# Row gathers that wait for TensorE's matrix products, and a six-tile lag of the adds into node sums

## The reference, cut to what matters

```python
alpha = jnp.einsum('ehd,hd->eh', h_src, a_src) + jnp.einsum('ehd,hd->eh', h_dst, a_dst)
enc = jax.nn.relu(edge_attr @ edge_W.T + edge_b).reshape(-1, H, D)
alpha = alpha + jnp.sum(enc * h_dst, axis=-1)
```

```python
for l in range(L):
    xl = h @ W[l] + b[l]
    ee = edge_attr @ We[l] + be[l]
    msg = norm * jax.nn.relu(xl[row] + ee)
    agg = jnp.zeros_like(xl).at[col].add(msg)
    conv = agg + jax.nn.relu(xl + root[l]) / deg[:, None]
```

## Time and profile before

| | us |
|---|---|
| median of 3 runs | 6056.12 |
| lowest, highest | 6053.90, 6076.91 |
| the profiled execution | 6070.75 |
| its span in the profile | 6069.0 |
| of it edge_scores, first to last gather | 64.8 to 855.2 |
| of it attention_sums | 976.0 to 1263.7 |
| of it the five edge loops of the graph layers | 1922.3 to 2635.7, 2686.0 to 3396.6, 3447.1 to 4165.4, 4215.5 to 4927.5, 4977.2 to 5689.1 |

### The profile page before, as it was taken

How to read it: one execution, slowest core, us unless ns; L and a number is a source line. 1 busy time by engine, 2 the same in 40 slices (tenths; PEclk the granted TensorE clock), 3 DMA queues, 4 the chain that set the end, 5 groups by cost and what they waited for, 6 DMA issues and landing times. The chain is left out here.

```text
span 6069.0 us, 97065 instructions
## 1 busy us (share of the span) xinstructions
PE 4321.2 (71%) x21956; PEld 3597.1 (59%) x21957; DVE 3000.5 (49%) x7137; ACT 2162.7 (36%) x4764; POOL 2953.9 (49%) x3174
## 2 busy tenths in 40 slices
PE   5667745869996767767677677776777757777678
PEld 4444434758885666656666566665666656666555
DVE  4444456662223554455545545545455555445644
ACT  2111115622222444434444344443444434444311
POOL 3545435823333555535555355553555535555233
PEclk8887877979998888878888788887888878888689
DMA  5555545735654444434444344443444434444332
GB/s 188 170 171 169 166 127 165 206 108 162 179 179 133 116 120 114 115 100 119 120 115 116 98 114 118 118 114 99 114 118 121 115 99 120 114 120 117 112 104 87
DMA packets 429338, 782.78 MB, mean 129 GB/s; under 512 B 212572, under 2 KB 269520, under 8 KB 412007
## 3 DMA queue, kind: packets, MB, share of 16 engines
q0 software_dynamic: 136704, 360.53, 22.1%
q1 hardware_dynamic: 281489, 402.18, 21.1%
q10 hardware_dynamic: 11094, 19.50, 1.1%
HBM read 669.16 MB, written 114.48 MB: 129 GB/s over the span
## 5 line engine op out<-in xcount | busy, mean ns | idle before, releaser
L1959 POOL DMA_INDIRECT g_g<-xl_table,g_idx x2080 | 1974.6, 949 | 1586.4 <-DVE g_onehot L2086 635.1
L2006 PE MATMUL g_b<-g_onehot,g_msg 128*128 128x128 f32 x8320 | 1384.0, 321 | 776.6 <-ACT g_msg L2065 491.8
L2006 PEld LDWEIGHTS g_b<-g_onehot,g_msg 128*128 128x128 f32 x8320 | 1312.8, 231 | 972.8 <-DVE agg L2094 755.3
L1993 PE MATMUL g_b<-g_we,g_ea 128*128 128x256 f32 x4160 | 1297.8, 442 | 273.4 <-DVE g_msg L2081 162.3
L2094 DVE TENSOR_TENSOR agg<-agg,g_b 128x256 f32 x2080 | 869.4, 418 | 1214.3 <-remote 706.2
L1993 PEld LDWEIGHTS g_b<-g_we,g_ea 128*128 128x128 f32 x4160 | 846.1, 226 | 406.9 <-DVE g_msg L2081 192.1
L2065 ACT ACTIVATE g_msg<-g_msg 128x512 f32<-128x512 f32 x1040 | 650.2, 625 | 1070.3 <-DVE g_msg L2081 881.5
L2081 DVE TENSOR_TENSOR g_msg<-g_g,g_b 128x512 f32<-128x512 f32 x1040 | 712.3, 685 | 567.9 <-PE g_b L1993 203.7
L543 PE MATMUL sc_pe_h<-ae_h_rows,sc_onehot 128*128 x1664 | 494.6, 448 | 243.6 <-DVE sc_prod L648 238.2
L511 POOL DMA_INDIRECT sc_g<-h_table,sc_idx x416 | 400.6, 963 | 390.7 <-DVE sc_prod L648 273.8
L543 PEld LDWEIGHTS sc_pe_h<-ae_h_rows,sc_onehot 128*128 128x128 f32 x1664 | 343.2, 217 | 351.0 <-issue 293.8
(11 more groups left out here) (306 smaller groups left out, 3694.0 us busy)
## 6 DMA issues: line engine op xcount, KB each, us to landing
g_ea<-in_ea SPq DMA_DIRECT2D x260, 512.0 KB
ex_w<-in_f_w SPq DMA_DIRECT2D x80, 1024.0 KB
e_rows<-sc_g SPq DMA_DIRECT2D x52, 1088.0 KB
at_g<-e_rows SPq DMA_DIRECT2D x104, 544.0 KB, 4.5
g_g<-xl_table,g_idx POOLq DMA_INDIRECT x2080
xl_table<-g_rows SPq DMA_DIRECT2D x25, 640.0 KB, 3.8
sc_rel<-rel_row ACTq DMA_DIRECT2D x52, 256.0 KB
sc_g<-h_table,sc_idx POOLq DMA_INDIRECT x416
```

Source lines behind the costliest of these rows:

```text
L1959: nc.gpsimd.indirect_dma_start(out=g.g[:, j, :], out_offset=None, in_=k.xl_table[:, :], in_offset=bass.IndirectOffsetOnAxis(ap=g.idx[:, q, ...
L1993: last = nc.tensor.matmul(ep[u % EB][:, i * D:(i + 1) * D], g.ea[:, q, (at + i) * P:(at + i + 1) * P], g.we[:], start=True, stop=True)
L2006: last = nc.tensor.matmul(ps[u % (SB // 2)][:, at:at + P], g.msg[:, j, b * P:(b + 1) * P], g.onehot[:, j, :], start=True, stop=True)
```

## The change

Three things change. In the graph layers POOL's gather of pair n waits for one counter, `summed` of pair n-4, in place of `raw` of n-5, `hot` of n-8 and `act_hot` of n-8. In edge_scores the gather of pair n waits for `expanded` of pair n-2 in place of `multiplied` of pair n-5, also in the first iteration from pair 2 on. LAG becomes 6: DVE adds the sums of the pair three behind, in the graph layers and, tile by tile, in attention_sums; the last LAG adds follow after the loop.

```diff
--- before.py
+++ after.py
@@ -39,8 +39,9 @@
 HROW = HEADS * (HD + 1)
 GROW = HROW + HEADS
 ACC = NP + P
-LAG = 4
-WINDOW = 5
+LAG = 6
+WINDOW = 4
+SCORE_WINDOW = 2
 LAYERS = 5
 XROW = D + 2
 PARTS = 3
@@ -503,9 +504,9 @@
                         pool.wait_ge(scored, it * 2 - 1 + q)
                         pool.wait_ge(kept[q], it * 16)
                 if not first:
-                    pool.wait_ge(multiplied, it * PAIRS + u - WINDOW + 1 + RING)
-                elif u >= WINDOW:
-                    pool.wait_ge(multiplied, u - WINDOW + 1 + RING)
+                    pool.wait_ge(expanded, it * PAIRS + u - SCORE_WINDOW + 1)
+                elif u >= SCORE_WINDOW:
+                    pool.wait_ge(expanded, u - SCORE_WINDOW + 1)
                 pool.sem_inc(begun, 1)
                 for j in (2 * u, 2 * u + 1):
                     nc.gpsimd.indirect_dma_start(
@@ -1966,7 +1967,7 @@
                 pool.wait_ge(g.idx_in[u // (HALF // 2)], l * (16 * ITERS) + 16)
                 pool.sem_inc(g.begun, 1)
             if u >= WINDOW:
-                pool.wait_ge(g.raw, u - WINDOW + 1 + EB)
+                pool.wait_ge(g.summed, 2 * (u - WINDOW + 1) + BODY)
                 pool.sem_inc(g.begun, 1)
             gather(u)
         with pool.Fori(1, ITERS) as it:
@@ -1974,9 +1975,7 @@
                 if u % (HALF // 2) == 0:
                     pool.wait_ge(g.idx_in[u // (HALF // 2)], it * 16 + l * (16 * ITERS) + 16)
 
-                pool.wait_ge(g.raw, it * (BODY // 2) + u - WINDOW + 1 + EB)
-                pool.wait_ge(g.hot, it * (BODY // 2) - BODY // 2 + u + 1)
-                pool.wait_ge(g.act_hot, it * (BODY // 2) - BODY // 2 + u + 1 + 2)
+                pool.wait_ge(g.summed, it * BODY + 2 * (u - WINDOW + 1) + BODY)
                 pool.sem_inc(g.begun, 1)
                 gather(u)
```

## The result

The changed kernel takes 5615.1 us (median of 4, 5607.9 to 5618.8) where the kernel before takes 6055.0 us on the same chip: a ratio of 0.9265, 95% interval 0.9241 to 0.9289. Forecast were 5732 us, the right way and too little: 440 us went, 323 were forecast. One thing has to be said at once, since the experiments turned on it: on other chips the kernel before takes 4889 us, and there the change makes it slower, by 1.1%.

A forecast was written before the change was run, and what follows sets the result against it. POOL's gather issue was taken as the floor, with stops for late PE reports above it. Terms -248 (wait on sums), -81 (edge_scores), +4 (LAG) gave -325: 6070.75 to 5746, less 0.24%, 5732 us; range 5400 to 6060.

The forecast's parts named there:

- What bounds the kernel: Gather loops: POOL's issue is the floor, 20.0 us per 16 gathers, PE just under at 19.5; waits above it 1173 us.
- the prediction's bound: Whole kernel: if all of POOL's stops went, -907 - 266 + 4, to 4890 us.
- The mechanism: Gather loops: POOL's own runs keep PE's reports back; POOL then stops because DVE, awaiting the report, hasn't raised the counter.
- The wait on sums: Graph layers: 6 gathers per stop at 1.9 us, 5.07 in place of 6.98 us an iteration, -248 us.
- LAG 6 at nothing: Graph layers: gain of the longer lag put at 0; without the new waits worth up to its "remote" idle.
- edge_scores: Its gather loop: 6 gathers per stop at 2.66 us, 7.1 in place of 10.2 us an iteration, -81 us.
- attention_sums and the tails: attention_sums: 287.7 us, change 0; two more adds ending each of 6 loops: +4 us.
- A (longer runs): Gather loops: 9 gathers or more between stops; with 9, 5451 us; 20% chance.
- B (too many stops): Gather loops: tight wait stops POOL too often; with 4 gathers per stop +96, to 6152 us; 8% chance.
- C: Gather loops: POOL isn't the cause, reports late whatever it does; slower, to 6278 us; 7% chance.
- D (no effect): Gather loops: another wait takes the stops over one for one; within 0.5% of 6056 us; 5% chance.

The follow-up runs named there:

- loop 10: Test-kernel graph-layer loop as before, SP's feature loads cut to 1/128, PE's matmuls to 8 and 16 columns, DVE's adds to 16 columns: 724 us, late chip.
- loop 1: Test-kernel graph-layer loop in the form of the kernel before, first of fourteen in one kernel: 746 us from first to last gather, late chip.
- loop 2: Test-kernel graph-layer loop as before with only LAG 6 in place of 4: 681 us from first to last gather, late chip.
- loop 4: Test-kernel graph-layer loop in the changed form, LAG 6 and the wait on sums n-4: 644 us from first to last gather, late chip.
- loop 5: Test-kernel graph-layer loop with LAG 6 and POOL waiting for DVE's raw of n-3 in place of n-5: 681 us, late chip.
- loop 3: Test-kernel graph-layer loop as before (lag 4) with only the wait on sums n-4: 670 us from first to last gather, late chip.
- the flaw of the loops with lag 4: Test-kernel loops with lag 4 read positions at a shifted place; DVE stands 3.7 us once an iteration, 2.5 us more, 63 us in all per loop.
- loop 14: Test-kernel graph-layer loop as before with a fill on POOL in place of each gather: 526 us, late chip.
- loops 8 and 10: Test-kernel loops as before: 8 with PE's matmuls cut to 8 and 16 columns, 741 us; 10 with loads and DVE's adds cut too, 724 us.
- fourteen forms: One test kernel with fourteen graph-layer edge loops, each in another form, on a late chip; the kernel before took 6061.3 us beside it.

## Why the prediction was right or wrong

**What bounds the kernel, right.** POOL's issue at 1.25 us a gather is the floor, and 1173 us above it are what late reports cost: shown by the prompt chips, where the same kernel takes 4889 us, the figure of the prediction's bound. PE's lower clock isn't what costs them: loop 10, at a granted clock of 0.50 and with PE's columns cut, is no slower than loop 1 at 0.80. The thought that lateness might be a trait of the chip, or of its state, didn't come up in the prediction, and that the changed kernel was timed on a late chip is luck: on a prompt one the same forecast would have met a slower kernel.

**The mechanism, half right.** "POOL's own runs keep PE's reports back" is shown in so far as fills in place of gathers take the late reports away on a late chip. It is wrong as a full cause: twelve gathers in a row beside a plain exchange of PE and DVE kept nothing back on such a chip. A further condition is open, and so is what makes a chip late.

**The wait on sums, right in kind, near in size.** Forecast were 6 gathers per stop at 1.9 us net, 5.07 us of idle time in an iteration. Counted in the timeline of the changed kernel (stops of more than 0.4 us) it is 6.1 gathers and 2.08 - 0.30 = 1.78 us; the first loop, 643.4 us from first to last gather, leaves (643.4 - 520) / 26 = 4.7 us. That is -60 us for a loop, where -50 were forecast. With the lag at 6 in both, the wait itself is worth 37 us of a loop (loops 2 and 4), and through DVE's counter it is worth nothing (loop 5).

**LAG 6 at nothing, not settled.** The reason given was: "once the runs are cut short, the report of two pairs back is in time too". It isn't always: in loop 3, with the wait and lag 4, DVE's adds wait 31.7 us for PE and 10.8 us on "remote", in loop 4, with lag 6, 3.2 us. Whether that costs time isn't shown. Loop 3 is 26 us longer than loop 4, but it carries the flaw of the loops with lag 4, and no run on a late chip has the wait without the lag in a whole kernel. Without the wait the lag alone seems worth some 20 us a loop, as far as loop 2 can be held against the kernel before; the prediction had allowed that it could be worth something there. So up to 5 x 26 = 130 of the 298 us that the five loops lost may be the lag's, and the size of the wait's term, 248 us, may have come out near in part by luck.

**edge_scores, under-sized.** Forecast were 6 gathers per stop (6.3 counted) and 2.66 us net for a stop. The stops last 2.3 us at the most common and 1.86 us in the mean, so 1.56 us net, and the idle time is 4.0 us in an iteration where 7.1 was forecast. What was too dear is, for the common stops, the 2.16 us from POOL's last gather to the report; the mean lies lower still because other stops are shorter. The gather ahead of the stop at 298.86 ends at 296.53, and DVE takes up PE's product here:

```profile
298.11 0.70 DVE L649 TENSOR_TENSOR sc_prod<-sc_enc,sc_pe_h 128x528 f32<-128x528 f32 x1 [2.38 <-PE sc_pe_h L544]
```

That is 1.6 us after it; it is the same at 286.04, 310.37 and 322.46. The 2.16 us had come from a run of 14 gathers, these stand behind runs of eight; that the length of the run makes the difference is likely and not shown. The loop lost 155 us where 81 were forecast. The price of a stop in edge_scores is thus the term that carries most of the miss: the spans differ by 463 us where 325 were forecast, and of these 138 us edge_scores has 74 and the five loops 50.

**attention_sums and the tails, right.** 287.7 us before and after; the tails cost at most the 0.2% that the lag alone costs on a prompt chip (9 us, 4 were forecast).

**The rivals.** A (longer runs) had a part in it: eight gathers between stops is common in both loops, yet the mean stays at six. B (too many stops) is seen with sums n-3: 4.0 gathers per stop, 683 us, which gives up 39 of the 60 us that the changed loop gained but doesn't end slower. C, as a mechanism of late reports without POOL's gathers, is excluded by loop 14. The rule of the Trainium skill's page "SBUF — State Buffer" in the part on its two sides, by which on the engines' side only DVE and GpSimd contend for a port, is about ports and not about reports. Loop 14 agrees with it: fills, which do write that memory, leave no "remote" wait. D (no effect) is excluded by the interval of 0.9241 to 0.9289. A change for the worse did exist, through a door that I hadn't looked at: where nothing is late, four pairs of lead are too few by 0.3 us an iteration, 8 us a loop, and the kernel is 1.1% slower.

## What to carry to other kernels

When an engine shows "remote" waits of several us on a counter whose producer had finished, look at what the issuer of gathers was doing. Shorten the lead of that issuer first: in edge_scores that alone gave 134 of 155 us. Where it gives nothing, as in the graph layers, let the issuer wait for the late producer itself. That the reports come through in the issuer's pause fits the rows of both loops. Work that depends on such a report can be put further back in the consumer's order; what that is worth here lies between 0 and 26 us a loop. Time such a change on more than one chip: here it is worth 7% on one and costs 1% on another, and a lead of five pairs in place of four does better on either. And check a test kernel against the kernel that it stands for, with a loop in the original form: here it showed that nine of fourteen forms carried a delay of their own.

## What the runs showed of the hardware

- The same kernel takes 4887 to 4889 us on some chips and 6055 to 6181 us on others, each steady within 0.6% in its own group. Chip number 10 stands for a prompt group and for a later, late one, so it may be a state rather than the part.
- On late chips PE's counter updates reach DVE and ACT several us late beside gathers in a row: in loop 1 PE's last sums end at 1799.24, and DVE, idle for 8.57 us, makes the add that waits for sums at 1808.18, 8.9 us after them and 3.1 us after POOL's last gather. It takes indirect gathers: 416 fills of 1.0 us in their place leave no "remote" wait. It stays with the columns of PE's matmuls and DVE's adds cut and with 1/128 of SP's feature loads.
- Twelve gathers in a row beside a hand-over of PE and DVE, on a late chip, kept nothing back: every tick 1.05 us.
- A wait for landing after every pair costs 41 us an iteration in place of 29: POOL then stands for 2.9 us in the mean at each pair, which is dearer than the late reports.
- PE at a granted clock of 0.50, with its columns cut, made these loops no slower (loops 8 and 10, 741 and 724 us, against 746 and 757).
